# Two batches' output projection kept transposed, and five reorderings at the two ends of a transformer block

## The chip, the cores and the metric

The kernel runs on one core of one Trainium2 chip. Its time is the device time of one execution in microseconds (us), and a version's time is the median of its runs. The core has TensorE (matrix products, PE in the profile), VectorE (DVE), ScalarE (ACT), GpSimd (POOL) and SyncE (SP), each with an instruction queue of its own, processed in order; semaphores alone hold one engine to another.

## What is computed

One pre-norm transformer layer on x of 4 batches x 1024 tokens x 128 channels, 16 heads of 64 channels:

```python
x = x + attn(layernorm(x))          # attn adds its own input: h + z, h = layernorm(x)
#   q, k, v = h @ w_q, h @ w_k, h @ w_v            per head
#   z = softmax(q k^T / 8) v, heads side by side, @ w_o
x = x + moe(layernorm(x))
#   router: softmax(xf @ Wr), one expert of 8 for each token, at most 512 tokens an expert
#   y = p * relu(xe @ W1[e]) @ W2[e], put back at the token's row
```

## The kernel before

**Attention.** The heads are done two at a time: a pair `j` (0 to 31, `LAST` = 31, eight pairs `HP` a batch) is worked in four parts called `oct`, two for each half `h` of 512 queries. In an oct TensorE makes eight score tiles (keys standing, 512 queries moving; lines 1367 and 1368) that ScalarE exponentiates into `ring` (L831), multiplies them with the values (`values`, L1383, 16 instructions), and makes two visits of plain scores for the next pair (`max_scores`, L1315). VectorE takes the maxima of these visits (`reduce_max`, L1054). GpSimd adds the exponentiated tiles up for the softmax sums (`add_up`, L662, seven additions of 128x1024 a half); TensorE turns them into sums with a product with ones (`softmax_sums`). VectorE inverts the sums (`recip`, L1059), and `scale_z` (L1068) multiplies z by them. In the last half of the last pair TensorE itself sums the last `LAST_BY_PE` = 2 tiles (`sums_by_pe`, L1391), and GpSimd adds the others.

**Output projection.** `project_out(j, h, bank)` (L1410) runs two pairs later, in octs 1 and 3 (one in each oct of the last pair): four products with a 128x128 tile of z standing and the 128x128 weights `wo` moving, which give rows of tokens. `add_out` (L1070, its addition L1074) adds that bank to the residual rows `x2`. PE's next visit waits for it (`wo_added`), as the bank is one half of the visit's bank. In oct 3 of a pair and in oct 1, `turn_max` (L1348) transposes the maxima behind it.

**The start.** VectorE takes the moments and the inverse roots of the first batch (`inverse_root`: a first guess and three Newton steps of three instructions, L947 to L949, each awaited by the next), then normalises; TensorE transposes and projects, and makes the first visits of pair 0 (`first_visit`) one by one as VectorE frees the banks. `turn_max(0, 0, ps_z)` follows `first_visit(4, 0)`.

**The end.** In `pair` of VectorE, `scale_z(LAST - 2, 0)` stands in oct 3 of pair 30, and `scale_z(LAST - 2, 1)` and `scale_z(LAST - 1, 0)` in oct 0 of the last pair behind the second two maxima. ScalarE's copy of the sums of pair 30 (`copy_sums_out`, L822) waits for the latter, as both use `sums`, and TensorE's third score tile of oct 1 waits for that copy, as the bank is the same. After the last pair TensorE makes router logits of the last batch's first half (L1437), runs `sums_by_pe`, `count_ranks` (L1478 to L1484), `softmax_sums` (L1406), then `end_project` and `end_turn_sums`; VectorE's `end_half(1)`, `end_root(1)` and `choose(B, ...)` follow, and with the slots found GpSimd scatters the last tokens (L632). TensorE meanwhile centres W1 (L1666), spins on products nobody reads (L1265) and transposes the first expert's tokens (L1679).

**The experts.** ScalarE casts the transposed tokens to the high part (`xeT_split`), VectorE makes the remainder (`low_tokens`, `xeT_ready`). For each of four chunks TensorE adds three products: low weights x high tokens, high weights x low tokens, high x high (L1705 to L1707), all behind `xeT_ready`.

What sets the order around the change is written out by hand: `pair` of each engine says what stands where in each oct.

Of the kernel before, what the change touches and what calls it, by code (L numbers as in the profile page):

```python
# [25 lines left out]
def block_kernel(nc, x_in, w_q, w_k, w_v, w_o, w_r, w_1, w_2, out):  # L26
# [31 lines left out]
    with ExitStack() as ctx:  # L58
# [62 lines left out]
        sums = sb("sums", [P, HALF])  # L121
        mxw = [sb(f"mxw{i}", [P, 2 * HT]) for i in range(2)]
# [79 lines left out]
        wo_added = sem("wo_added")  # L202
        sums_turned = sem("sums_turned")
# [92 lines left out]
        LAST_BY_PE = 2  # L296
# [70 lines left out]
        assert all(ROUTE_FROM + 2 * b >= HP * (b + 1) + 1 for b in range(1, B - 1)) and ROUTE_FROM + 2 * B + 2 <= PAIRS  # L367

# [565 lines left out]
        def _(dve):  # L934
# [11 lines left out]
            def newton(v, y, t):  # L946
                then(dve.scalar_tensor_tensor(out=t, in0=y, scalar=-0.5, in1=y, op0=ALU.mult, op1=ALU.mult))  # L947
                then(dve.tensor_tensor(t, t, v, ALU.mult))
                return dve.scalar_tensor_tensor(out=y, in0=t, scalar=1.5, in1=y, op0=ALU.add, op1=ALU.mult)  # L949
# [15 lines left out]
            def inverse_root(n, c):  # L965
# [4 lines left out]
                for _ in range(3):  # L970
                    then(newton(v, y, t))
# [134 lines left out]
            def end_root(h):  # L1106
# [4 lines left out]
                then(newton(v, y, t))  # L1111
                then(newton(v, y, t))

            def end_root_done(h):
                n, c = 2 * B - 1, slice(h * HT, (h + 1) * HT)
                v, y, t = (roots[:, n, k, c] for k in range(3))
                newton(v, y, t).then_inc(root_ready, 1)
# [8 lines left out]
            def pair(j, par, b):  # L1126
                nxt = 1 - par
                first, last = known(j, 0), known(j, LAST)
                for oct in range(OCTS):
# [19 lines left out]
                    if oct >= 2 and not known(j, LAST - 1, LAST):  # L1149
                        low_qk(j + 2, oct - 2)  # L1150
                    if outputs(j, oct) is not None:
                        add_out(*outputs(j, oct), lent_out)
# [105 lines left out]
        def _(pe):  # L1258
# [229 lines left out]
            def pair(j, par, b):  # L1488
# [3 lines left out]
                for oct in range(OCTS):  # L1492
# [38 lines left out]
                    for made in tiles:  # L1531
                        if made[2] is not lent_max:
                            project_tile(*made)
                    if outputs(j, oct) is not None:
# [199 lines left out]
```

## Time and profile before

| | |
|---|---|
| median of 3 runs | 1509.79 us (1508.08 to 1510.36) |
| the profiled execution | 1508.29 us, its span 1506.2 us |
| busy share PE, POOL, DVE, ACT | 98%, 81%, 66%, 52% |
| chain that ended last | PE 87%, POOL 5%, DVE 3%, issue 2% |
| granted clock of TensorE, mean | 0.995 |

A row of the trace's timeline gives start and duration in us, engine, line, operation, tiles and the count of merged instructions; the brackets give idle time of that engine before it and who ended it. An f32 product is two instructions in these records (x8 for the four products of `project_out`), one with both operands f32r is one. Durations of neighbouring products overlap, so what a product costs is read from starts.

### The profile page before, as it was taken

The page shows a single profiled execution, that of the slowest core. Times are in us where ns is not written, and L with a number is a line of the kernel's source. Part 1 is how long each engine was busy: PE and PEld are TensorE (multiplying, and loading weights), DVE is VectorE, ACT ScalarE, POOL GpSimd, SP SyncE. Part 2 cuts the span into 40 slices and gives each one's busy share as a digit, 9 for nine tenths or more (in the row PEclk, how much of TensorE's full clock was granted, in tenths as well). Part 3 has the DMA queues.
Part 4 walks back from the last instruction along what each step waited for, and adds up shares of the span by engine and source line. Part 5 has one row for each costly group of instructions (what it writes and reads, how often), then busy time and mean ns, then how long its engine had stood idle before and what let it go on. Part 6 is the DMA issues. An engine that isn't in the chain of part 4 may idle for free.

```text
span 1506.2 us, 21680 instructions
## 1 busy us (share of the span) xinstructions
PE 1478.4 (98%) x7244; PEld 841.6 (56%) x7244; DVE 995.8 (66%) x1228; ACT 784.5 (52%) x1540; POOL 1216.1 (81%) x675
## 2 busy tenths in 40 slices
PE   8999999999999999999999999999999999998897
PEld 5555555555555555555555555555655556554586
DVE  6557666676777656766666657676677666677543
ACT  4565556565555554555455555555555455453331
POOL 5888778898798878888778878889789998899535
PEclk9999999999999999999999999999999999999999
DMA  6334444442343434332444433333444423440431
GB/s 149 90 81 93 94 113 108 107 104 60 82 104 88 114 83 108 87 83 65 95 98 100 114 83 90 86 76 89 98 96 96 107 72 79 103 107 12 133 84 34
DMA packets 125294, 137.88 MB, mean 92 GB/s; under 512 B 44107, under 2 KB 69198, under 8 KB 125185
## 3 DMA queue, kind: packets, MB, share of 16 engines
q1 hardware_dynamic: 118784, 130.26, 37.3%
q0 software_dynamic: 2048, 4.10, 0.9%
q10 hardware_dynamic: 4352, 2.13, 0.5%
q8 instruction: 59, 0.97, 0.3%
q14 instruction: 51, 0.41, 0.1%
HBM read 16.81 MB, written 8.45 MB: 17 GB/s over the span
## 4 chain that ended last, share of the span: by engine, by line
PE 87%; POOL 5%; DVE 3%; issue 2%; ACT 1%; SPq 1%; DMA 1%; POOLq 0%; ACTq 0%; DVEq 0%
PE ps_w L1383 27%; PE ps_w L1367 16%; PE ps_w L1368 14%; PE ps_m L1315 10%; POOL acc L662 4%; PE ps_m L1416 3%; PE ps_w L1401 2%; PE ps_m L1283 2%; PE ps_m L1284 2%; PE ps_m L1285 2%; DVE mxw L1054 1%; PE ps_w L1690 1%; DVE z L1068 1%; PE ps_m L1690 1%; PE ps_m L1300 1%
## 5 line engine op out<-in xcount | busy, mean ns | idle before, releaser
L662 POOL TENSOR_TENSOR acc<-acc,ring 128x1024 f32<-128x1024 f32 x382 | 918.9, 2406 | 50.9 <-ACT ring L831 3.3
L1054 DVE TENSOR_REDUCE mxw<-ps_m 128x1 f32<-128x1024 f32 x512 | 601.4, 1217 | 323.3 <-PE ps_m L1315 312.3
L831 ACT ACTIVATE ring<-ps_w 128x512 f32<-128x512 f32 x1024 | 544.8, 600 | 253.5 <-PE ps_w L1368 235.9
L1383 PE MATMUL ps_w<-ring,V 128*64 128x512 f32 x2048 | 467.7, 598 | 0.0
L1367 PE MATMUL ps_w<-queriesA,keysA 128*128 128x512 f32 x1024 | 431.9, 422 | 5.1 <-ACT sums L822 2.8
L1368 PE MATMUL ps_w<-queriesB,keysB 65*128 65x512 f32 x1024 | 406.9, 397 | 0.0
L1383 PEld LDWEIGHTS ps_w<-ring,V 128*64 128x64 f32 x2048 | 135.7, 136 | 265.5 <-issue 234.9
L662 POOL TENSOR_TENSOR acc<-ring 128x1024 f32<-128x1024 f32 x64 | 152.2, 2378 | 157.4 <-PE ps_w L1401 150.5
L1367 PEld LDWEIGHTS ps_w<-queriesA,keysA 128*128 128x128 f32 x1024 | 194.0, 189 | 106.1 <-issue 48.6
L1368 PEld LDWEIGHTS ps_w<-queriesB,keysB 65*128 65x128 f32 x1024 | 194.7, 190 | 33.6 <-issue 0.7
L1315 PE MATMUL ps_m<-keysA,queriesA 64*128 64x512 f32 x1000 | 183.0, 444 | 1.2 <-issue 0.5
L1315 PEld LDWEIGHTS ps_m<-keysA,queriesA 64*128 64x128 f32 x1000 | 74.5, 184 | 149.6 <-issue 138.2
L811 ACT ACTIVATE z<-ps_w 128x512 f32<-128x512 f32 x64 | 38.3, 598 | 217.6 <-PE ps_w L1383 217.6
L1045 DVE TENSOR_TENSOR qk_rest<-ps_m,qk_high 128x512 fp32r<-128x512 f32 x123 | 85.1, 692 | 93.1 <-ACT qk_high L769 81.3
L1059 DVE RECIPROCAL sums<-sums 128x128 f32<-128x128 f32 x128 | 119.7, 940 | 0.0
L822 ACT ACTIVATE sums<-ps_w 128x512 f32<-128x512 f32 x33 | 19.7, 598 | 126.4 <-PE ps_w L1401 112.1
L1068 DVE TENSOR_TENSOR z<-by_sums,z 128x512 f32<-128x512 f32 x60 | 79.2, 1325 | 0.0
L769 ACT ACTIVATE qk_high<-ps_m 128x512 fp32r<-128x512 f32 x123 | 73.6, 598 | 8.7 <-DMA keysB<-qk_high 1.5
L1416 PEld LDWEIGHTS ps_m<-wo,z 128*128 128x128 f32 x496 | 65.8, 193 | 7.2 <-DVE mxw L1054 1.9
L1416 PE MATMUL ps_m<-wo,z 128*128 128x128 f32 x496 | 66.4, 277 | 1.1 <-DVE mxw L1054 1.1
L695 POOL DMA_INDIRECT out<-ye,ring x32 | 31.1, 971 | 35.2 <-DVE ye L1230 28.2
L1074 DVE TENSOR_TENSOR x<-ps_m,x 128x512 f32<-128x512 f32 x62 | 42.7, 688 | 23.5 <-PE ps_m L1416 23.5
(181 smaller groups left out, 981.3 us busy)
## 6 DMA issues: line engine op xcount, KB each, us to landing
queriesA<-qk_high SPq DMA_DIRECT2D x248, 128.0 KB
keysB<-qk_high SPq DMA_DIRECT2D x124, 128.0 KB
keysA<-qk_rest SPq DMA_DIRECT2D x124, 128.0 KB
queriesB<-qk_rest SPq DMA_DIRECT2D x124, 128.0 KB
by_sums<-sums SPq DMA_DIRECT2D x240, 64.0 KB, 2.0
keysA<-qk_high SPq DMA_DIRECT2D x93, 128.0 KB
tokens_by_slot<-blank ACTq DMA_DIRECT2D x16, 130.0 KB, 3.1
ring<-tokens_by_slot SPq DMA_DIRECT2D x8, 260.0 KB, 5.3
```

The costliest lines, as they stand in the source:

```text
L662: pool.tensor_tensor(acc[h][:, :], before, P_both(kt), ALU.add).then_inc(summed, 1)
L769: act.activation(qk_high[s][:, :], bank, ACT.Copy).then_inc(qk_cast, 1)
L831: act.activation(P_tile(kt, p), ps_s[k % 3][:, :], ACT.Exp, scale=SCALE).then_inc(exp_done, 1)
L1045: dve.tensor_tensor(qk_rest[s][:, :], qk_bank(j, use), qk_high[s][:, :].bitcast(F32), ALU.subtract).then_inc(qk_low, 1)
L1054: dve.tensor_reduce(mxw[h][:, p * HT + qt:p * HT + qt + 1], ps_m[p][:, :], AX_X, ALU.max).then_inc(maxed, 1)
L1059: dve.reciprocal(sums[:, c], sums[:, c]).then_inc(recip_done, 1)
L1068: dve.tensor_tensor(z[j % 2][h][:, :], by[:, :], z[j % 2][h][:, :], ALU.mult).then_inc(z_ready, 1)
L1315: mm = pe.matmul(ps_m[p][:, kh * HALF:(kh + 1) * HALF], queriesA[par][p][r, at:at + P], keysA[par][p][r, kh * HALF:(kh + 1) * HALF], start ...
L1367: pe.matmul(ps_s[k % 3][:, :], keysA[par][p][:, t], queriesA[par][p][:, c], start=True, stop=False)
L1368: pe.matmul(ps_s[k % 3][:, :], keysB[par][p][:, t], queriesB[par][p][:, c], start=False, stop=True).then_inc(scores_ready, 1)
L1383: mm = pe.matmul(ps_z[p * DK:(p + 1) * DK, :], V_of(j, kt, p), P_tile(kt, p), start=(kt == 0), stop=(kt == KT - 1))
L1416: mm = pe.matmul(bank[:, i * P:(i + 1) * P], z[j % 2][h][:, i * P:(i + 1) * P], wo[j % 3][:, :], start=True, stop=True)
```

## The change

1. **Output projection.** For pairs whose batch is 1 or 2 and that aren't the last of their batch (14 pairs, 28 halves), `project_out` makes one product with `wo` standing and 512 columns of z moving. The result is out transposed; VectorE sums it in `outT`, a view of `h_rows`, the first by a copy. In pairs 17 and 25, octs 1 and 2, `turn_back` (four transposes, by TensorE) turns a half of the sum and `add_back` (VectorE) adds it to the residual rows. The batch's last pair is added directly, behind `add_back`.
2. **`LAST_BY_PE`** is 1; after the last pair `softmax_sums` stands ahead of `count_ranks`.
3. **Roots.** Three Newton steps become one step of third order (four instructions) and one of second order (three), at the start and in `end_root`.
4. **`scale_z`** moves: for (29, 0) from oct 3 to oct 2 of pair 30; (29, 1) and (30, 0) ahead of the second two maxima of the last pair's oct 0.
5. **First visits.** `turn_max(0, 0, ps_z)` stands ahead of `first_visit(4, 0)`.
6. **Experts.** The two products with high tokens stand ahead of the one with low tokens; for expert 0 those of three chunks run ahead of the wait for `xeT_ready`.

```diff
-        LAST_BY_PE = 2
+        LAST_BY_PE = 1
+        outT = h_rows[:, :, :].rearrange("p t d -> p (t d)")
+        def transposed(j):
+            return 0 < j // HP < B - 1 and j % HP < HP - 1
+        def back(j, oct):
+            b, pair = divmod(j - HP - 1, HP)
+            return (b, oct - 1) if pair == 0 and 0 < b < B - 1 and oct in (1, 2) else None
...
-            def newton(v, y, t):
+            def third_order(v, y, t):
+                then(dve.tensor_tensor(t, y, y, ALU.mult))
                 then(dve.tensor_tensor(t, t, v, ALU.mult))
+                then(dve.scalar_tensor_tensor(out=t, in0=t, scalar=-10.0 / 3.0, in1=t, op0=ALU.add, op1=ALU.mult))
+                then(dve.scalar_tensor_tensor(out=y, in0=t, scalar=5.0, in1=y, op0=ALU.add, op1=ALU.mult))
+            def second_order(v, y, t):
+                ...
+                # three instructions, as newton had
...
             def add_out(j, h, bank):
                 b = j // HP
                 dve.wait_ge(wo_done, out_no(j, h))
+                if transposed(j):
+                    at = outT[:, h * HALF:(h + 1) * HALF]
+                    if j % HP > 0:
+                        dve.wait_ge(wo_added, out_no(j, h) - 2)
+                        dve.tensor_tensor(at, bank, at, ALU.add).then_inc(wo_added, 1)
+                    else:
+                        if b == 1:
+                            dve.wait_ge(residual_ready, B)
+                            dve.wait_ge(h_turned, 2 * B)
+                        else:
+                            dve.wait_ge(back_turned, 2 * b - 2)
+                        dve.tensor_copy(at, bank).then_inc(wo_added, 1)
+                    return
+                if 0 < b < B - 1:
+                    dve.wait_ge(back_added, 2 * b + h - 1)
+            def add_back(b, g):
+                dve.wait_ge(back_turned, 2 * b + g - 1)
+                dve.wait_ge(residual_ready, b + 1)
+                at = x_tiles(b, g * HT, HT)
+                dve.tensor_tensor(at, lent_turn.rearrange("p (t d) -> p t d", d=D), at, ALU.add).then_inc(back_added, 1)
...
+                    if last and oct == 0:
+                        scale_z(j - 2, 1)
+                        scale_z(j - 1, 0)
                     if oct == 2 and not (first or last or both):
                         recip(j - 1, 1, 3)
                     if not (last and oct >= 1):
...
                         reduce_max(v, h, qt, 1)
                         reduce_max(v, h, qt, 0)
-                    if oct == 0 and last:
-                        scale_z(j - 2, 1)
-                        scale_z(j - 1, 0)
-                    if oct == 3 and known(j, LAST - 1):
+                    if oct == 2 and known(j, LAST - 1):
                         scale_z(j - 1, 0)
...
+                if transposed(j):
+                    pe.matmul(bank, wo[j % 3][:, :], z[j % 2][h][:, :], start=True, stop=True).then_inc(wo_done, 1)
+                    return
...
+            def turn_back(b, g):
+                pe.wait_ge(wo_added, 2 * HP * (b + 1) - 2)
+                for i in range(g * HT, (g + 1) * HT):
+                    mm = pe.transpose(lent_turn[:, (i - g * HT) * P:(i - g * HT + 1) * P],
+                                      outT[:, i * P:(i + 1) * P], ident[:, :])
+                mm.then_inc(back_turned, 1)
...
-            first_visit(4, 0)
             pe.wait_ge(first_copied, 4)
             turn_max(0, 0, ps_z)
+            first_visit(4, 0)
...
             sums_by_pe(LAST, 1, range(KT - LAST_BY_PE, KT))
+            softmax_sums(LAST, 1, LAST_BY_PE)
             count_ranks(B - 1, lent_out)
-            softmax_sums(LAST, 1, LAST_BY_PE)
...
             for e in range(E):
+                ahead = 3 if e == 0 else 0
+                pe.wait_ge(xeT_split, e + 1)
+                for c in range(ahead):
+                    up_by_high(e, c)
                 pe.wait_ge(xeT_ready, e + 1)
                 for c in range(FC):
+                    if c >= ahead:
+                        up_by_high(e, c)
+                    up_by_low(e, c)
```

## Rows read from the trace of the kernel before

**Rows 1.** The page: busy time, share and instructions of each engine.
```profile
PE 1478.4 (98%) x7244; PEld 841.6 (56%) x7244; DVE 995.8 (66%) x1228; ACT 784.5 (52%) x1540; POOL 1216.1 (81%) x675
```

**Rows 2.** Timeline of PE: start, duration, engine, line, operation, tiles, count.
```profile
42.34 1.02 PE L1279 MATMUL ps_m<-hT,wst 128*128 128x512 f32 x2
...
43.43 0.40 PE L1368 MATMUL ps_w<-queriesB,keysB 65*128 65x512 f32 x1
...
443.17 0.40 PE L1368 MATMUL ps_w<-queriesB,keysB 65*128 65x512 f32 x1
443.41 0.60 PE L1270 MATMUL ps_m<-ident,h_rows 128*128 128x128 f32 x4
...
444.08 0.39 PE L1368 MATMUL ps_w<-queriesB,keysB 65*128 65x512 f32 x1
...
1396.99 1.05 PE L1416 MATMUL ps_m<-wo,z 128*128 128x128 f32 x8
...
1398.12 0.40 PE L1368 MATMUL ps_w<-queriesB,keysB 65*128 65x512 f32 x1
```

**Rows 3.** Timeline of PE, the last pair's octs 0 and 1.
```profile
1372.97 1.16 PE L1416 MATMUL ps_m<-wo,z 128*128 128x128 f32 x8 [1.05 <-DVE mxw L1054]
...
1385.21 0.50 PE L1367 MATMUL ps_w<-queriesA,keysA 128*128 128x512 f32 x1 [2.76 <-ACT sums L822]
```

**Rows 4.** Timeline of ACT in the last pair.
```profile
1384.56 0.60 ACT L822 ACTIVATE sums<-ps_w 128x512 f32<-128x512 f32 x1 [8.31 <-DVE z L1068]
```

**Rows 5.** Timeline of DVE from pair 30 to the last pair's oct 1.
```profile
1367.39 1.65 DVE L1068 TENSOR_TENSOR z<-by_sums,z 128x512 f32<-128x512 f32 x1
...
1378.50 3.19 DVE L1068 TENSOR_TENSOR z<-by_sums,z 128x512 f32<-128x512 f32 x1
1381.62 2.84 DVE L1068 TENSOR_TENSOR z<-sums,z 128x512 f32<-128x512 f32 x1
```

**Rows 6.** The instructions of line 1068: count, ns min/median/max, first and last start.
```profile
L1068 DVE TENSOR_TENSOR z<-by_sums,z x60: 678/1273/3193, 118.9 to 1378.5; 128x512 f32<-128x512 f32 x60
```

**Rows 7.** Timeline of POOL in the last pair.
```profile
1373.93 0.99 POOL L632 DMA_INDIRECT tokens_by_slot<-x,scatter_at  x1 [0.16 <-issue]
...
1378.77 2.37 POOL L662 TENSOR_TENSOR acc<-ring 128x1024 f32<-128x1024 f32 x1
1381.28 15.75 POOL L662 TENSOR_TENSOR acc<-acc,ring 128x1024 f32<-128x1024 f32 x6
1397.42 2.38 POOL L662 TENSOR_TENSOR acc<-ring 128x1024 f32<-128x1024 f32 x1 [0.40 <-ACT ring L831]
```

**Rows 8.** Busy time by stretch, us of PE, PEld, DVE, ACT, POOL, then PEclk.
```profile
1385.00:1391.00 6.00, 5.79 (x23) 4.51 (x25) 4.52 (x6) 3.96 (x9) 5.71 (x3) 0.72 0.00 0
```

**Rows 9.** Timeline of PE behind the last pair and at the first expert.
```profile
1414.42 1.06 PE L1437 MATMUL ps_m<-wr_centred,hT 128*128 128x8 f32 x8
1415.41 1.94 PE L1391 MATMUL ps_w<-ring,ones 128*64 128x512 f32 x8
...
1417.55 1.08 PE L1406 MATMUL ps_w<-acc,ones 128*64 128x512 f32 x4
...
1441.89 0.47 PE L1705 MATMUL ps_w<-xeT_high,w_low 128*128 128x512 f32 x1 [1.50 <-DVE xeT_low L1236]
```

**Rows 10.** Timeline of DVE behind the last pair.
```profile
1420.02 0.21 DVE L1082 RECIPROCAL end_scale<-ps_w 128x8 f32<-128x8 f32 x1 [0.96 <-PE ps_w L1447]
...
1425.31 0.16 DVE L949 SCALAR_TENSOR_TENSOR roots<-roots 128x4 f32<-128x4 f32 x1
1425.51 0.19 DVE L1001 TENSOR_REDUCE routing_columns<-ps_m 128x4 f32<-128x32 f32 x1
```

**Rows 11.** Timeline of PE at the start.
```profile
9.86 0.66 PE L1270 MATMUL ps_w<-ident,h_rows 128*128 128x128 f32 x4 [1.47 <-DVE h_rows L975]
...
28.47 0.73 PE L1326 MATMUL ps_m<-keysA,queriesA 64*128 64x512 f32 x2
29.13 0.50 PE L1367 MATMUL ps_w<-queriesA,keysA 128*128 128x512 f32 x1
```

More of the change, by code:

```diff
@@ L202, in block_kernel @@
         wo_added = sem("wo_added")
+        back_turned = sem("back_turned")
+        back_added = sem("back_added")
         sums_turned = sem("sums_turned")
@@ L944, in then @@
                 dve.wait_ge(chain, steps[0])
-            def newton(v, y, t):
-                then(dve.scalar_tensor_tensor(out=t, in0=y, scalar=-0.5, in1=y, op0=ALU.mult, op1=ALU.mult))
+            def third_order(v, y, t):
+                then(dve.tensor_tensor(t, y, y, ALU.mult))
                 then(dve.tensor_tensor(t, t, v, ALU.mult))
-                return dve.scalar_tensor_tensor(out=y, in0=t, scalar=1.5, in1=y, op0=ALU.add, op1=ALU.mult)
+                then(dve.scalar_tensor_tensor(out=t, in0=t, scalar=-10.0 / 3.0, in1=t, op0=ALU.add, op1=ALU.mult))
+                then(dve.scalar_tensor_tensor(out=y, in0=t, scalar=5.0, in1=y, op0=ALU.add, op1=ALU.mult))
+            def second_order(v, y, t):
+                left = 3.0 / 8.0
+                then(dve.scalar_tensor_tensor(out=t, in0=y, scalar=-0.5 * left ** 3, in1=y, op0=ALU.mult, op1=ALU.mult))
+                then(dve.tensor_tensor(t, t, v, ALU.mult))
+                return dve.scalar_tensor_tensor(out=y, in0=t, scalar=1.5 * left, in1=y, op0=ALU.add, op1=ALU.mult)
             def find_moments(n, b, g):
@@ L969, in inverse_root @@
                 then(dve.tensor_scalar(y.bitcast(I32), v.bitcast(I32), -0.5, float(0x5F3759DF), ALU.mult, ALU.add))
-                for _ in range(3):
-                    then(newton(v, y, t))
+                third_order(v, y, t)
+                then(second_order(v, y, t))
             def first_norm(g):
@@ L1110, in end_root @@
                 then(dve.tensor_scalar(y.bitcast(I32), v.bitcast(I32), -0.5, float(0x5F3759DF), ALU.mult, ALU.add))
-                then(newton(v, y, t))
-                then(newton(v, y, t))
+                third_order(v, y, t)
             def end_root_done(h):
@@ L1150, in pair @@
                         low_qk(j + 2, oct - 2)
+                    if back(j, oct) is not None:
+                        add_back(*back(j, oct))
                     if outputs(j, oct) is not None:
@@ L1533, in pair @@
                             project_tile(*made)
+                    if back(j, oct) is not None:
+                        turn_back(*back(j, oct))
                     if outputs(j, oct) is not None:
@@ L1573, in pair @@
                             pe.wait_ge(hT_ready, 2 * turn[0] + turn[1] + 1)
+                        if back(j, oct) is not None:
+                            b, g = back(j, oct)
+                            pe.wait_ge(back_added, 2 * b + g - 1)
                         if c is not None and oct < 2:
@@ L1697, in _, with up_by_high, up_by_low @@
             pe.wait_ge(w2_loaded, 16 * FC)
+            def up_by_high(e, c):
+                n, w = e * FC + c, slice(e * F + c * P, e * F + (c + 1) * P)
+                if n >= 3:
+                    pe.wait_ge(relu_done[(n - 3) % 2], (n - 3) // 2 + 1)
+                pe.matmul(up_bank(n), w1_low[:, w], xeT_high[e % 2][:, :], start=True, stop=False)
+                pe.matmul(up_bank(n), w1_high[:, w], xeT_high[e % 2][:, :], start=False, stop=False)
+            def up_by_low(e, c):
+                n, w = e * FC + c, slice(e * F + c * P, e * F + (c + 1) * P)
+                pe.matmul(up_bank(n), w1_high[:, w], xeT_low[e % 2][:, :], start=False,
+                          stop=True).then_inc(up_done, 1)
             for e in range(E):
+                ahead = 3 if e == 0 else 0
+                pe.wait_ge(xeT_split, e + 1)
+                for c in range(ahead):
+                    up_by_high(e, c)
                 pe.wait_ge(xeT_ready, e + 1)
                 for c in range(FC):
[L1701 to L1708 removed]
+                    if c >= ahead:
+                        up_by_high(e, c)
+                    up_by_low(e, c)
                 if e + 1 < E:
```

10 lines of the change are left out of this document (1 added, 9 removed).

## The prediction

> **What bounds the kernel now.** I read the busy shares first: TensorE (PE) is busy for 1478.4 of 1506.2 us [rows 1], so through most of the kernel a change is worth what it takes from PE's own stream. POOL stands second at 81%, which matters where PE becomes faster. Then I looked at what PE's stream costs in the middle, by distances between starts [rows 2], and then for the places where PE waits. These lie at the two ends. In the last pair PE waits 1.05 us for VectorE's maxima and 2.76 us for a copy by ScalarE [rows 3]; that copy had itself waited 8.31 us for `scale_z` [rows 4]. Behind the wait the granted clock is 0.72 of full over 6 us [rows 8], so part of that stretch ran at 1.2 instead of 2.4 GHz.
>
> **The wide projection, 28 times.** Three places are measured in the same way, from the start of the special product to the start of the second score product (L1368) behind it. For the narrow form it is 1398.12 - 1396.99 = 1.13 us [rows 2]. The wide form isn't in this kernel as an output projection, but `project_qk` of pair 1 is the same shape, 128x128 f32 standing and 512 f32 columns moving: 43.43 - 42.34 = 1.09 us [rows 2]. One projection thus gains 0.04 us, 28 gain 1.1 us. The reason is that both forms stream 512 columns in two instructions' worth of passes, and four small products pay hardly anything for their weight loads. Bounds of the wide price: 0.41 us lower if it took only as long as two f32r products of 512 columns (443.41 - 443.17 = 0.24 each [rows 2], 0.48 against 0.89 for the narrow set, which is 1.13 less one such 0.24), and as high as two whole durations, bounded by the first product's 1.02 us in the row of L1279 against that 0.89, 0.13 higher. I take 1.09, the row of equal shape.
>
> The Trainium skill (TensorE: Matmul & The Clock Gate, section Back-to-back issue gap) has streams of a weight load and a product each at about 81 ns for 128 columns and 131 ns for 512, which would make wide products far cheaper by the column. By it, as an estimate, eight narrow instructions are 0.65 us, two wide ones 0.26, and 28 projections would give 10.8 us instead of 1.1. The trace doesn't agree: its eight narrow ones take 0.89 us and its two wide ones 0.85.
>
> **Turning back, 4 times.** Four transposes by identity, measured alike: 444.08 - 443.41 = 0.67 us, less the 0.24 of the score product that lies between: 0.43 us [rows 2]. Four of them cost PE 1.7 us. With each comes an `add_back` on DVE, an addition with one PSUM operand that I price as `add_out`'s, 0.7 us. In octs 1 and 2 of pairs 17 and 25 it is queued ahead of `add_out` or `scale_z`, a reciprocal and two maxima; PE's next visit waits for it. DVE is 66% busy [rows 1], and PE itself reaches the visit 0.43 us later, so I take no wait; if DVE's queue has no room there, it is up to 0.7 each, 2.8 in all. The waits that `add_out` gains are for adds two places back, and once, in pair 10, for POOL's residual of batch 3, which is queued ahead of that pair's first addition; I take nothing for them. The middle: -1.1 + 1.7 = +0.6 us, bounds -9.8 (cheap wide products) and +8.1 (0.13 x 28 + 1.7 + 2.8).
>
> **`scale_z` in pairs 30 and 31.** Its price depends on POOL. Over 60 instances the least is 0.68 us and the median 1.27 [rows 6]; the two in the last pair took 3.19 and 2.84 [rows 5], under POOL's additions, which run on from 1378.77 [rows 7]. (a) `scale_z(29, 0)` took 1.65 us [rows 5] ahead of two reciprocals and the maxima for which PE then waited 1.05 us [rows 3]. Moved one oct up it is off that path, and DVE waits for PE's visits there, so it is hidden: -1.05 us. (b) The other two now stand behind `add_out` at 1373.7 (my shifted time) and ahead of the maxima. In that time, 1373.93 to 1378.77, POOL issues four scatters and adds nothing [rows 7], so I take 0.7 to 1.3 us each. They end at about 1376, the maxima behind them at 1378.6, and PE asks for these after `values` and the sums, at 1379.4. If both took 3 us, PE would wait some 2.5 us there. (c) The copy of the sums then finds z scaled, and PE's wait of 2.76 us [rows 3] goes. What is late next is the product of the sums itself, which ends before oct 1. (d) With the gap gone I expect the low clock behind it to go too: 6 x (1 - 0.72) = 1.7 us [rows 8]. Sum of the last pair: 1.05 + 2.76 + 1.7 = 5.5 us, so that `values` of the last oct end at 1414.42 - 5.5 = 1408.9 [rows 9].
>
> **POOL, now next.** POOL doesn't move with this: its additions of the first half run without a gap to 1397.03, its second half began after 0.40 us of waiting [rows 7], which goes. With `LAST_BY_PE` = 1 it has six additions instead of five, at 2.5 (1381.28 - 1378.77) to 2.62 us (15.75/6) [rows 7]: from about 1397.0 to 1412.2. PE needs one tile of sums less (half of 1.94 us) and would be ready at 1408.9 + 1.0 + 1.0 = 1410.9. So `softmax_sums` starts when POOL is done, 1412.2 against 1417.55 [rows 9]: -5.3 us, of which the reorder with `count_ranks` and the smaller `sums_by_pe` can show no more, because POOL ends last. `count_ranks` (0.27 us, from 1417.28 in the trace to 1417.55) now lies between the sums and `end_turn_sums`, for which `end_half(1)` waited [rows 10]: +0.2.
>
> **Roots.** Two instructions fewer at 0.20 us of spacing [rows 10]. In `end_root(1)` the logits' `choose` follows them at once [rows 10]: -0.4. In `end_root(0)` DVE waits for the logits afterwards: 0. At the start PE waits 1.47 us for the normalised rows [rows 11]: -0.4.
>
> **First visits.** The scores of pair 0 start right behind the last visit (28.47, 29.13, no idle time [rows 11]), and the visits wait for VectorE, not for `turn_max`: 0. If the placed maxima ended as late as the visits, up to 0.6.
>
> **Experts.** PE waited 1.50 us for the low tokens [rows 9]; some 0.8 of it, VectorE's subtraction and its signal, is now covered by six products. But the first chunk is complete only after seven products instead of three, and the fourth chunk needs its bank back from the relu: 0.3 to 0.5 us of it return. -0.3, from 0 to -0.7. The later experts wait as before.
>
> **Sum.** +0.6 - 5.3 + 0.2 - 0.4 - 0.4 - 0.3 = -5.6 us. The profiled execution took 1508.3 us, which gives 1502.7; the median of the runs is 1.5 us above that execution. I put the forecast between the two bases, at 1503.3.
>
> **Rivals.** *The last pair pays half.* (b) goes wrong: scaling in front of the maxima still meets POOL, PE waits 2.5 us for the second visit, and that gap keeps part of the low clock. For it: 3.19 and 2.84 in the trace. Against it: the scatters lie just there. Gain 5.6 - 2.5 = 3.1 and less, 1506.0. *The wide product is dearer than equal shape says*, at its bound of 0.13 more than narrow, and `add_back` finds no room: the middle costs 8.1, 7.5 more than forecast: 1510.8. It changes the sign when a wide product costs 0.2 us more than I take (5.6/28). This is the slower case; for it speaks only that the row of L1279 is from the start, against it that PE streams columns everywhere at the same pace. With half of that price the result is near zero. *The wide product is cheap*, as two f32r products: 28 x 0.41 = 11.5 instead of 1.1, so 1492.9. For it no row; the rule of the skill quoted above points there. *The order doesn't do what it says*: VectorE's moved steps change nothing, because the last pair is tied to POOL's additions already. Against it, POOL's sums of the first half end at 1397.03, and PE would need them at 1397.3. If POOL were 1 to 2 us slower, PE would wait there, but then `softmax_sums` at the end is later by the same: 1505.
>
> **How the numbers follow.** Forecast 0.66; half pay or POOL slower 0.17 (1505 to 1506); middle dearer by half 0.07 (about 1508); dearer in full 0.05; cheap wide products 0.05. A measurement of this kernel can tell about 0.2%, 3.0 us, from no change. Faster by more than that: most of the forecast (0.64), half of the second case (0.08), the cheap case (0.05): 0.76 with rounding. Slower: 0.06. Within: 0.18. The range is 1499.5 to 1507.5: the terms at their good ends (first visits 0.6, experts 0.4, less low clock at W1, the profile's base) below, the half paying case and the higher base above; it leaves out the cheap case and the two dear ones.
>
> **What would show it.** In the profile after: L1416 with x2 at 128x512 taking the same distance to the second L1368 (1.09 us), not 0.7 or 1.3; four sets of transposes from `outT` at 0.43; no 2.76 us wait of L1367 for `sums`, and no low clock near 1386; L1068 at 0.7 to 1.3 in the last pair's oct 0; POOL's last addition ending right before L1406; PE's wait at the first expert near 0.7. I am wrong if the middle, from 300 to 1330 us, is shorter or longer by over 2 us, or if L1406 behind the last pair starts less than 4 us earlier.

## The result, and the profile after

The changed kernel takes 1506.29 us (median of 20 runs, 1502.63 to 1510.25). The kernel before, run beside it, takes 1508.51 us (20 runs, 1506.41 to 1514.71). The ratio is 0.9978, 95% interval 0.9971 to 0.9986: faster by 2.1 to 4.4 us. It lies near the ratio of the means (1505.94 and 1509.13 us); the medians are only 2.2 us apart. The profiled execution took 1507.38 us, with a span of 1505.5 us. The forecast was 1503.3 us, a gain of 5.6 against the base of the sum. The direction is right and the time lies inside the range, but more than two of the forecast microseconds are missing. The trace shows where each went.

Busy times, from the page of the kernel after (compare rows 1):

```profile
PE 1479.8 (98%) x7088; PEld 826.5 (55%) x7088; DVE 1002.3 (67%) x1226; ACT 784.5 (52%) x1540; POOL 1217.6 (81%) x676
```

PE has 156 instructions fewer and is as busy as before. The count alone doesn't give the time here.

**The last pair.** The timeline of PE after (start, duration, engine, line, operation, tiles, count, and in brackets the idle time before with what ended it):

```profile
1379.41 0.73 PE L1361 MATMUL ps_m<-keysA,queriesA 64*128 64x512 f32 x4
1380.07 3.65 PE L1429 MATMUL ps_w<-ring,V 128*64 128x512 f32 x16
1383.55 1.03 PE L1452 MATMUL ps_w<-acc,ones 128*64 128x512 f32 x4
1384.51 0.73 PE L1361 MATMUL ps_m<-keysA,queriesA 64*128 64x512 f32 x4
1385.17 0.50 PE L1413 MATMUL ps_w<-queriesA,keysA 128*128 128x512 f32 x1
```

No row of it has an idle time in brackets. Before, there was one of 1.05 and one of 2.76 us [rows 3]. VectorE over the same time, and ScalarE's copy of the sums:

```profile
1378.12 0.69 DVE L1113 TENSOR_TENSOR x<-ps_m,x 128x512 f32<-128x512 f32 x1 [1.25 <-PE ps_m L1465]
1378.72 0.82 DVE L1092 TENSOR_TENSOR z<-by_sums,z 128x512 f32<-128x512 f32 x1
1379.47 0.68 DVE L1092 TENSOR_TENSOR z<-sums,z 128x512 f32<-128x512 f32 x1
1380.17 2.36 DVE L1078 TENSOR_REDUCE mxw<-ps_m 128x1 f32<-128x1024 f32 x2
```
```profile
1384.63 0.60 ACT L837 ACTIVATE sums<-ps_w 128x512 f32<-128x512 f32 x1 [4.43 <-PE ps_w L1452]
```

The two scalings take 0.82 and 0.68 us instead of 3.19 and 2.84 [rows 5]. ScalarE now waits for PE's product, no longer for z [rows 4]. The low clock behind the gap is gone: busy times of PE, PEld, DVE, ACT and POOL with their counts, then PEclk, DMA share and GB/s, which answer to rows 8:

```profile
1384.00:1390.00 6.00, 6.00 (x33) 3.99 (x29) 4.33 (x5) 3.98 (x9) 5.70 (x4) 1.00 0.03 11
```

I compared the starts of `values` oct by oct in both traces. The shift between them falls by 1.27 us at the last pair's oct 0 and by 4.50 us at its oct 1: 5.77 us, where the forecast had 1.05 and 2.76 + 1.7 (5.5 in all).

**Behind the last pair.** PE after (compare rows 9):

```profile
1413.88 1.06 PE L1493 MATMUL ps_m<-wr_centred,hT 128*128 128x8 f32 x8
1414.87 1.08 PE L1437 MATMUL ps_w<-ring,ones 128*64 128x512 f32 x4
1416.94 1.08 PE L1452 MATMUL ps_w<-acc,ones 128*64 128x512 f32 x4 [1.00 <-POOL acc L677]
1418.88 0.19 PE L1534 MATMUL ps_m<-one_hot_b,upper 128*128 128x32 bf16 x1 [0.85 <-DVE one_hot_b L1031]
```

The wait of 1.00 us for POOL was forecast: POOL ends last. The wait of 0.85 us for the one-hots wasn't. VectorE shows where it comes from, in `end_root(0)`, and POOL what runs beside it:

```profile
1410.88 1.05 DVE L1154 TENSOR_SCALAR roots<-moments 128x4 f32<-128x4 f32 x1
1411.96 0.17 DVE L1155 TENSOR_SCALAR roots<-roots 128x4 int32<-128x4 int32 x1
1412.16 2.25 DVE L964 TENSOR_TENSOR roots<-roots 128x4 f32<-128x4 f32 x1
1414.45 0.16 DVE L965 TENSOR_TENSOR roots<-roots 128x4 f32<-128x4 f32 x1
1414.64 2.27 DVE L966 SCALAR_TENSOR_TENSOR roots<-roots 128x4 f32<-128x4 f32 x1
1416.94 0.16 DVE L967 SCALAR_TENSOR_TENSOR roots<-roots 128x4 f32<-128x4 f32 x1
...
1417.62 0.19 DVE L1025 TENSOR_REDUCE routing_columns<-ps_m 128x4 f32<-128x32 f32 x1
```
```profile
1404.49 12.40 POOL L677 TENSOR_TENSOR acc<-acc,ring 128x1024 f32<-128x1024 f32 x5
```

An instruction on 128x4 elements takes 0.16 us, except three: the first takes 1.05 us, and two later ones take 2.25 and 2.27 us. Before, these roots ran while POOL had already finished, and all of them took 0.16 or 0.17:

```profile
1413.72 0.16 DVE L949 SCALAR_TENSOR_TENSOR roots<-roots 128x4 f32<-128x4 f32 x1
1415.52 0.19 DVE L1001 TENSOR_REDUCE routing_columns<-ps_m 128x4 f32<-128x32 f32 x1 [1.64 <-PE ps_m L1437]
```

So the roots had 1.64 us of room before, and now they are late. The product of the ranks starts 5.00 us behind the start of the logits (2.86 before), and the first W1 product 13.50 us (12.59 before): 0.9 us lost.

**The middle.** A wide product next to a set of turning products, and then PE and DVE at the first turning back (pair 17, octs 2 and 3):

```profile
1079.98 1.02 PE L1462 MATMUL ps_m<-z,wo 128*128 128x512 f32 x2
1080.85 0.60 PE L1480 MATMUL ps_m<-ident,x 128*128 128x128 f32 x4
```
```profile
788.00 0.60 PE L1472 MATMUL ps_m<-ident,h_rows 128*128 128x128 f32 x4
788.36 0.48 PE L1413 MATMUL ps_w<-queriesA,keysA 128*128 128x512 f32 x1
...
795.16 0.73 PE L1361 MATMUL ps_m<-keysA,queriesA 64*128 64x512 f32 x4 [0.91 <-DVE mxw L1078]
```
```profile
788.66 0.68 DVE L1119 TENSOR_TENSOR x<-ps_m,x 128x512 f32<-128x512 f32 x1
789.26 2.78 DVE L1092 TENSOR_TENSOR z<-by_sums,z 128x512 f32<-128x512 f32 x1
791.96 0.94 DVE L1083 RECIPROCAL sums<-sums 128x128 f32<-128x128 f32 x1
792.83 2.28 DVE L1078 TENSOR_REDUCE mxw<-ps_m 128x1 f32<-128x1024 f32 x2
```

The two instructions of one wide product take 1080.85 - 1079.98 = 0.87 us. The octs with one are shorter than before, by up to 0.05 us each; over the 28 this is 0.9 us (0.45 in pairs 10 to 16 and 0.42 in pairs 18 to 24, read in proj_only, which has no other change), where 1.1 was forecast. The turning costs more than forecast: the shift between the traces grows by 0.44, 0.27 and 0.96 us over octs 1 to 3 of pair 17, and by the same amounts in pair 25, 3.3 us in all instead of 1.7. `add_back` itself takes 0.68 us, as forecast (0.7). But it pushes `scale_z` to where that takes 2.78 us, and PE waits 0.91 us for the maxima behind it. The addition of POOL that `scale_z` meets there begins 0.15 us ahead of it:

```profile
789.11 2.38 POOL L677 TENSOR_TENSOR acc<-acc,ring 128x1024 f32<-128x1024 f32 x1
```

**Phases of low clock.** The shift also jumps by 3.05 us in pair 24, and this is no wait:

```profile
1091.84 0.95 PE L1493 MATMUL ps_m<-wr_centred,hT 128*128 128x8 f32 x8
...
1093.44 0.60 PE L1414 MATMUL ps_w<-queriesB,keysB 65*128 65x512 f32 x1
...
1095.97 5.77 PE L1429 MATMUL ps_w<-ring,V 128*64 128x512 f32 x16
```
```profile
1093.70:1100.50 6.80, 6.80 (x19) 2.26 (x20) 4.44 (x15) 1.49 (x3) 6.51 (x4) 0.52 0.05 13
```

For 6.8 us PE is busy throughout, but at the lower of its two levels (1.2 GHz; the granted clock is 0.52 of full), and `values` takes 5.77 us instead of 3.65. A shorter phase at 18 us (3.4 us) takes back the 0.48 us that the roots gave at the start and 1.1 more. Whether such phases belong to the change was the first thing to settle.

**The experts.** PE waits 0.78 us instead of 1.50 [rows 9], and 0.32 us come back behind the ninth product, ahead of the fourth chunk:

```profile
1441.70 0.47 PE L1763 MATMUL ps_w<-xeT_high,w_low 128*128 128x512 f32 x1 [0.78 <-ACT xeT_high L934]
...
1444.35 0.50 PE L1763 MATMUL ps_w<-xeT_high,w_low 128*128 128x512 f32 x1 [0.32 <-DVE rT L1296]
```

### The profile page after: what moved, and what is told of

The parts are those of the page before. It is cut to its first block, busy times and chain, and to the rows that moved or that the text cites. A ratio compares the mean times of both kernels' runs of the same rounds, so it can differ in the third digit from the quotient of the medians.

```text
span 1505.5 us, 21408 instructions
## 1 busy us (share of the span) xinstructions
PE 1479.8 (98%) x7088; PEld 826.5 (55%) x7088; DVE 1002.3 (67%) x1226; ACT 784.5 (52%) x1540; POOL 1217.6 (81%) x676
## 4 chain that ended last, share of the span: by engine, by line
PE 90%; DVE 4%; POOL 2%; ACT 1%; issue 1%; DMA 0%; POOLq 0%; ACTq 0%; DVEq 0%
PE ps_w L1429 28%; PE ps_w L1413 17%; PE ps_w L1414 15%; PE ps_m L1361 10%; POOL acc L677 2%; PE ps_w L1447 2%; PE ps_m L1465 2%; PE ps_m L1329 2%; PE ps_m L1330 2%; PE ps_m L1331 2%; PE ps_m L1462 2%; DVE mxw L1078 1%; PE ps_w L1751 1%; PE ps_m L1751 1%; PE ps_m L1346 1%
## 5 line engine op out<-in xcount | busy, mean ns | idle before, releaser
L1329 PE MATMUL ps_m<-h_high,w_low 128*128 128x512 f32 x120 | 47.6, 397 | 0.0
L1330 PE MATMUL ps_m<-h_low,w_high 128*128 128x512 f32 x120 | 47.3, 394 | 0.0
L1331 PE MATMUL ps_m<-h_high,w_high 128*128 128x512 f32 x120 | 47.2, 394 | 0.0
```

What stands on the lines that cost most here:

```text
L1329: pe.matmul(bank, w_low[par][:, w], h_high[:, c], start=True, stop=False)
L1330: pe.matmul(bank, w_high[par][:, w], h_low[:, c], start=False, stop=False)
```

## The experiments

Ten kernels ran, in three groups, each with runs of the kernel before beside it: medians 1509.5, 1510.12 and 1508.59 us. The mean granted clock of one execution scatters between 0.988 and 0.996, and within a kernel the span follows it, by 1.06 us per 0.001 (a line with one slope through all executions but one; the one left out, of proj_only, had a clock of 0.944 and a span of 1528.3 us, and would not lie on it). So beside each ratio I give the span read from that line at a clock of 0.994, "at equal clock". The kernel before has 1505.9 +- 0.1 us there, the changed kernel 1503.3 +- 0.2.

Such a figure takes away chance, but also what a change does to the clock itself. The phase of low clock behind the old gap in the last pair is in all four traces that have the old order of the scalings (the kernel before, before_again, proj_only, experts_only; 3.4 us, in proj_only 6.8) and in none of the eight with the new order, where PEclk is 1.00 from 1378 to 1396 us. 3.4 us at half clock are 1.7 us, or 0.0011 of the mean clock; by the line that is 1.2 us. As an estimate, the kernels with the new order are thus some 1.2 us better against the kernel before than their figures at equal clock say.

**before_again** is the kernel before, unchanged.

> The kernel before, unchanged, for the granted clock of each of its executions. Theory A (phases of low clock fall on any version, by where TensorE's idle and thin stretches happen to lie): ratio 1.000, the mean granted clock scatters between 0.991 and 0.996 from execution to execution, and the span follows it, about 1.5 us for each 0.001. Theory B (the change brought the extra low phases of the after trace, at 18 us and at 1094 us): the clock here is 0.995 in all executions, with the scatter of the spans unrelated to it.

Measured: 1508.77 us, ratio 0.9998 [0.9988, 1.0009], 1505.9 at equal clock. Its clocks reach from 0.990 to 0.995, nearly as far as those of the changed kernel, with spans from 1504.7 to 1511.6 us: theory A in that. The span follows less steeply than expected, 1.06 us per 0.001 and not 1.5. The trace itself shows no phase in the middle; its one at 1386 us (PEclk 0.57 over 1386 to 1390) is that of the gap in the last pair.

**ends_only** has the changes of order, and the projection as before (the diff is against the changed kernel):

```
         def transposed(j):
-            return 0 < j // HP < B - 1 and j % HP < HP - 1
+            return False
...
         def back(j, oct):
...
-            return (b, oct - 1) if pair == 0 and 0 < b < B - 1 and oct in (1, 2) else None
+            return None
...
-                if 0 < b < B - 1:
-                    dve.wait_ge(back_added, 2 * b + h - 1)
```

> The changed kernel with the output projection as it was before (no transposed sums, no turning back); the five reorderings stay. Theory A: the projection costs TensorE's stream 28 x -0.04 + 2 x 1.67 = +2.2 us, so this one is 2 us faster than the changed kernel, about 0.9965 of before; from pair 10 to pair 26 the distance to before stays constant. Theory B (the wide product is what keeps the clock down): also free of low phases in the middle, 0.9945. Rival C (the projection pays after all, by something the steps don't show): slower than the changed kernel, 0.998 or more.

Measured: 1502.87 us, ratio 0.9952 [0.9939, 0.9966], 1501.9 +- 0.5 at equal clock. The order alone gives more than the whole change: the two intervals don't meet. The ratio can't decide between A (0.9965) and B (0.9945), as its interval holds both. The trace speaks against B: it, too, has a phase of low clock in the middle, at 1091.5 us (PEclk 0.50 over 1091.5 to 1098), almost where the changed kernel has one, and it has neither wide products nor turning.

**proj_only** has the projection, and the order of before (all five edits at the ends undone).

> The kernel before with only the output projection changed. Theory A: +2.2 us by the steps of the trace (-0.04 in each oct with a wide product, +1.67 in each of pairs 17 and 25), ratio 1.0015. Forecast of the prediction: +0.6 us. Rival C: faster than before by 1 us or more.

Measured: 1511.53 us, ratio 1.003 [1.0004, 1.0056], 1507.9 +- 0.2 at equal clock: 2.0 us slower than before. By the steps in the trace it should be 3.3 - 0.9 = 2.4, and between pair 10 and pair 26 the trace's shift grows by 2.1. So eight of its ten executions need no effect on the clock to explain them. The other two stand out: 1517.78 us at a clock of 0.988 and 1530.28 us at 0.944, lower than any other execution on record. Neither was profiled, the 20 executions of the changed kernel, which has the same projection, reach no lower than 0.989, and why these two were so low is open.

**turn_late** is the changed kernel with the second turning back one oct later:

```
-            return (b, oct - 1) if pair == 0 and 0 < b < B - 1 and oct in (1, 2) else None
+            return (b, oct // 2) if pair == 0 and 0 < b < B - 1 and oct in (1, 3) else None
```

> The changed kernel with the second half turned back in oct 3 instead of oct 2. Theory A1 (in oct 2 the added step of VectorE pushes scale_z into GpSimd's next addition, where it takes 2.8 instead of 1.3 us, and the maxima behind it hold up TensorE's second visit by 0.91 us): pairs 17 and 25 cost 0.9 us each instead of 1.67, the wait of 0.91 us for the maxima is gone, 1.5 us less in all. Rival A2 (the turn costs what it costs wherever it is put): 1.67 each again, with the wait in oct 3.

Measured: 1504.83 us, ratio 0.9968 [0.9957, 0.9979], 1502.6 +- 0.3 at equal clock. In pairs 17 and 25 the steps of octs 1 to 3 are 0.44, -0.03 and 0.45 us: 0.87 a pair, twice PE's own 0.43, instead of 1.67. By its ratio alone it can't be told from the changed kernel; the trace decides. Its VectorE in the place of the rows above:

```profile
789.30 0.85 DVE L1092 TENSOR_TENSOR z<-by_sums,z 128x512 f32<-128x512 f32 x1
790.08 0.94 DVE L1083 RECIPROCAL sums<-sums 128x128 f32<-128x128 f32 x1
791.05 2.36 DVE L1078 TENSOR_REDUCE mxw<-ps_m 128x1 f32<-128x1024 f32 x2
```

This execution runs 0.64 us later there, POOL's additions with it. So `scale_z`, without an addition in front of it, starts 0.31 us before a running addition of POOL ends (789.61), and takes 0.85 us; in the changed kernel it started 0.15 us after the next one began. The extra 0.8 us a pair is thus VectorE's queue in oct 2 (theory A1), and most of what the addition does there is to push the scaling into POOL's next addition.

**scale_only** is the kernel before with the three scalings moved and nothing else:

```
+                    if last and oct == 0:
+                        scale_z(j - 2, 1)
+                        scale_z(j - 1, 0)
                     ...
-                    if oct == 0 and last:
-                        scale_z(j - 2, 1)
-                        scale_z(j - 1, 0)
-                    if oct == 3 and known(j, LAST - 1):
+                    if oct == 2 and known(j, LAST - 1):
```

> The kernel before with only the three moved steps of scale_z. Theory D (these moves are nearly the whole gain, and nothing behind the last pair takes it back as long as TensorE sums two tiles): values of the last pair's octs 0 and 1 come 1.26 and 5.76 us earlier, L1406 still starts 3.1 us behind the logits, ratio about 0.996. Rival E (GpSimd's additions take the gain back whatever LAST_BY_PE is): the logits are 5.8 us earlier, but L1406 starts over 4 us behind them, ratio 0.998.

Measured: 1503.3 us, ratio 0.9958 [0.9942, 0.9973], 1502.3 +- 0.6 at equal clock. The steps are -1.27 and -4.50 us, those of the changed kernel to the hundredth. The three moved lines give as much as all the changes of order in ends_only (0.9952) can be shown to give, and more than the whole change (theory D). One part of D was missed: L1406 starts 3.55 us behind the logits, between the 3.1 of D and the 4 of E. The roots of `end_root(0)` already meet POOL here, since everything of PE is earlier and POOL isn't: the ranks start 3.28 us behind the logits, and W1 13.00.

**pe2** is the changed kernel with `LAST_BY_PE` = 2.

> The changed kernel with LAST_BY_PE = 2 as before. Theory F (GpSimd's sixth addition keeps VectorE's instructions of end_root(0) waiting, 2.25 and 2.27 us for two of 0.16, so that the one-hots, the ranks and end_half(1) are late): GpSimd ends 2.5 us earlier, 0.5 us behind the start of the logits instead of 3.0; end_half(1) starts 5.7 to 5.9 us behind them instead of 6.7; 0.8 us faster than the changed kernel. Rival G (the order of softmax_sums and count_ranks is what costs): end_half(1) stays at 6.7, no gain, as TensorE has 0.9 us more to sum.

Measured: 1505.2 us, ratio 0.9969 [0.9956, 0.9982]. Its PE behind the last pair:

```profile
1412.39 1.06 PE L1493 MATMUL ps_m<-wr_centred,hT 128*128 128x8 f32 x8
1413.38 1.94 PE L1437 MATMUL ps_w<-ring,ones 128*64 128x512 f32 x8
1415.14 1.03 PE L1452 MATMUL ps_w<-acc,ones 128*64 128x512 f32 x4
1416.10 0.19 PE L1534 MATMUL ps_m<-one_hot_b,upper 128*128 128x32 bf16 x1
```

Both waits are gone, and POOL ends 0.52 us behind the start of the logits, as expected. From the logits to W1 it is 12.44 us instead of 13.50, so in the trace the sixth addition costs 1.1 us (theory F). The line at equal clock gives 1504.4 +- 0.7 and can't show so little.

**ends_pe2** is ends_only with `LAST_BY_PE` = 2.

> All that the steps of the traces say pays: the five reorderings with LAST_BY_PE = 2, and the output projection as it was. By theory A and F together: 2.1 us (projection) and 0.8 us (GpSimd) faster than the changed kernel, ratio to before 0.9948. If the parts don't add up (rival): 0.997, as the changed kernel.

Measured: 1503.88 us, ratio 0.9959 [0.9945, 0.9973], 1501.1 +- 0.5 at equal clock. In the trace W1 starts 12.23 us behind the logits, 1.3 earlier than in ends_only (13.52). By the ratios the two can't be told apart, and the interval holds both the expected 0.9948 and the rival's 0.997.

**experts_only** is the kernel before with the new order of the first expert's products.

> The kernel before with only the experts' order changed. Prediction: from the first transposes of tokens to the last product 0.3 us less than the 55.8 to 56.4 us of the kernel before; the wait for the first expert 0.8 instead of 1.5 us, a new one of 0.3 us in front of the fourth chunk. Rival: it is worth more, 0.7 us and over, because the later experts gain too.

One execution, 1509.15 us. PE waits 0.78 and 0.32 us there as in the changed kernel, and from the turning of the tokens to the last product it is 55.67 us. The other kernels with the old order have 56.44 (before), 55.75, 55.77 and 55.88, those with the new order 55.14 to 55.76. The gain of the wait, 1.50 - 0.78 - 0.32 = 0.4 us, is there; over the whole stretch it is no more than this scatter.

**split_add** and **ends_split** test what holds the tiny instructions up. POOL's additions of the last half are issued as two of half the width, in the changed kernel and in ends_pe2:

```
+                if known(j, LAST) and h == 1:
+                    half = slice(0, HALF)
+                    pool.tensor_tensor(acc[h][:, half], before[:, half], P_both(kt)[:, half], ALU.add)
+                    half = slice(HALF, 2 * HALF)
+                    pool.tensor_tensor(acc[h][:, half], before[:, half], P_both(kt)[:, half],
+                                       ALU.add).then_inc(summed, 1)
+                    return
```

> The changed kernel with POOL's additions of the last pair's second half (L677, 128x1024, 2.48 us each) issued as two of 128x512. Theory H: a VectorE instruction that reads two operands from SBUF waits for the end of POOL's running addition and is not slowed otherwise. Then no instruction of the first end root takes 2.25 us any more, but at most 1.3 (half an addition plus its own 0.16); there are more such waits, about one for each two root instructions; the roots are done about 6.0 us behind the start of the last logits instead of 6.8 less the logits, and the product of count_ranks starts at 4.0 to 4.6 us behind the logits instead of 5.00. POOL ends 0 to 0.5 us later (3.0 to 3.5 behind the logits). Rival R: two engines share the bandwidth, so a VectorE instruction beside an addition is slowed by a factor whatever the addition's length: then instructions of 2.2 us remain and count_ranks stays at 5.0. Median ratio to before 0.997 to 0.9985 in either case: this run is for the trace.

> The changes of order without the wide projection, two tiles of sums left to TensorE, and POOL's additions of the last pair's second half halved as in the other run. POOL ends at 0.6 to 1.0 us behind the start of the last logits (0.64 with whole additions). Theory H: the one wait of 2.25 us in the first end root becomes one or two of at most 1.3, count_ranks starts at 3.2 to 3.7 (3.72 before it), and the run gains 0 to 0.5 us on that of whole additions (ratio 0.9959): 0.9950 to 0.9960. Rival R: nothing moves.

Measured for split_add: 1505.27 us, ratio 0.9976 [0.9964, 0.9989]. VectorE and POOL:

```profile
1408.38 1.19 DVE L1162 TENSOR_SCALAR roots<-roots 128x4 int32<-128x4 int32 x1
1409.61 0.16 DVE L971 TENSOR_TENSOR roots<-roots 128x4 f32<-128x4 f32 x1
1409.81 1.17 DVE L972 TENSOR_TENSOR roots<-roots 128x4 f32<-128x4 f32 x1
1411.01 1.19 DVE L973 SCALAR_TENSOR_TENSOR roots<-roots 128x4 f32<-128x4 f32 x1
1412.24 0.16 DVE L974 SCALAR_TENSOR_TENSOR roots<-roots 128x4 f32<-128x4 f32 x1
```
```profile
1408.28 1.27 POOL L681 TENSOR_TENSOR acc<-acc,ring 128x512 f32<-128x512 f32 x1
1409.69 1.27 POOL L679 TENSOR_TENSOR acc<-acc,ring 128x512 f32<-128x512 f32 x1
1410.92 1.26 POOL L681 TENSOR_TENSOR acc<-acc,ring 128x512 f32<-128x512 f32 x1
1412.33 1.27 POOL L679 TENSOR_TENSOR acc<-acc,ring 128x512 f32<-128x512 f32 x1
```

The held instructions end at 1409.57, 1410.98 and 1412.20 us; POOL's additions end at 1409.55, 1410.96 and 1412.18. None takes over 1.19 us. A slowdown by a shared rate would have left some at 2.2. So theory H holds in this: such an instruction is held to the end of the addition that runs. The expected gain did not come. The rows show why: between the two halves of one tile POOL leaves no gap (1410.96 to 1410.92), and only behind the second one of 0.14 us (1409.55 to 1409.69, 1412.18 to 1412.33). The free instructions, L971 and L974, are the ones that start in such a gap. So there are five waits after the first instruction instead of two, the roots are no earlier, and the ranks start 5.22 us behind the logits (expected 4.0 to 4.6). POOL ends 0.8 us later for its twelve instructions. ends_split: 1504.59 us, ratio 0.9968 [0.9955, 0.9981], 1501.1 +- 0.1 at equal clock, the ranks at 3.72 as with whole additions. Its expectation of 0.9950 to 0.9960 was missed by the ratio. At equal clock it is level with ends_pe2: nothing gained, nothing lost, which is what rival R had said, though not for R's reason.

The three best ratios are those of ends_only, scale_only and ends_pe2: 0.9952, 0.9958 and 0.9959 against 0.9978 for the changed kernel. All three beat the kernel before; that they beat the changed kernel is clear of noise for ends_only only, as the other two intervals just reach its own.

## Why the prediction was nearly right, step by step

**The last pair was right, by its mechanism and by its size.** -5.5 forecast, -5.77 measured, and scale_only shows that the three moved lines do it alone. The two scalings met the last 0.27 us of an addition of POOL and its scatters (0.82 and 0.68 us; 0.7 to 1.3 forecast), and the low clock behind the gap went with the gap, in all eight traces without it.

**The wide product was right to the hundredth.** 0.04 us each was taken from the row of equal shape [rows 2], and 0.03 was measured, 0.9 us for the 28. The section Back-to-back issue gap of the Trainium skill (TensorE: Matmul & The Clock Gate) would have had, as an estimate from its figures, 10.8 us for the 28. The trace of the kernel after disagrees with it as that of before did: two instructions of 512 f32 columns take 0.87 us, four of 128 take 0.43.

**Turning back was mis-sized: 1.7 us forecast, 3.3 measured.** PE's part was right (0.43 a set, as turn_late's steps show). The term that failed is "PE itself reaches the visit 0.43 us later, so I take no wait". It used VectorE's mean busy share (66%) for one place. At that place the addition pushed `scale_z` from where it took 1.30 us to where it took 2.78, and with it the maxima. The 0.7 us for each turning, given there as a bound, is what oct 2 cost: 0.8 in each of the two pairs, 1.6 us in all.

**POOL as the next bound was right, and the roots behind it were overlooked.** That PE would wait for POOL at the sums is in the trace with 1.00 us. "In `end_root(0)` DVE waits for the logits afterwards: 0" is the step that failed. That room (1.64 us) existed because POOL had finished 3.64 us before the logits. With PE 5.8 us earlier in the last pair, and POOL with one addition more, POOL adds until 3.01 us behind their start, and the roots are held for 1.05 - 0.16 + 2.25 - 0.16 + 2.27 - 0.16 = 5.1 us. I had named that price in the same text for `scale_z` and didn't ask which other VectorE instructions would now run beside POOL. Cost: the forecast has W1 as far behind the logits as before (-5.5 at the logits, and -5.3 + 0.2 - 0.4 = -5.5 at W1), and the trace has it 0.9 us farther.

**The start was right in the wait (-0.48 us; -0.4 forecast), the experts in theirs (-0.4; -0.3).**

**The sum.** The forecast -5.6, with 1.6 more for the turning, 0.9 more at W1 and 0.2 more for the wide products, and with 0.3 less in the last pair and 0.1 less each at the start and the experts, is -3.4 us. The ratio says -3.3 (0.0022 x 1508.5), the line at equal clock -2.6 +- 0.3, or -3.8 with the 1.2 of the gap's own phase. The forecast time is off by 3.0 us: 2.3 by the gain, and 1.1 because the medians lie only 2.2 us apart and not 3.3, less 0.4 because the base was put at 1508.9 and came out at 1508.51.

**What was luck.** The time lies inside the range, but not by what the range allowed for. Its upper part, to 1507.5, stood for the last pair paying half and for the higher base; the last pair paid in full, and the two terms that came out dearer, the turning and the roots, were not in it. By the time alone, 1506.29, the rival at 1505 to 1506 would look right, and none of its mechanisms happened. Two of the signs of being wrong also show in the profiled execution as they are written: the middle is 4.2 us longer, and the product of the sums starts only 0.6 us earlier. 3.05 us of both are the low clock of pair 24, and the second also has the phase at 18 us in it. Without it the middle is 1.2 us longer, which would pass, and counted from the last pair on the product of the sums is 5.8 us earlier.

**What the clock did.** A comparison of the two profiled executions alone would have misled: they had clocks of 0.995 and 0.992, and at 1.06 us per 0.001 this is 3.2 us. The largest part of it in the two traces are the 3.05 us of pair 24. A phase in the middle is in three of the twelve traces: the changed kernel, turn_late (from 1180 us on) and ends_only (1091.5 us), so it needs no wide product. No kept trace with the old order has one there; that it falls on the kernel before too is inferred from the scatter of its clocks (0.990 to 0.995) and not shown. The phase near 18 us is shown on both: it is in eight of the twelve traces, and three of them (proj_only, scale_only, experts_only; PEclk 0.50 or 0.51 over 3.4 us) have the start of the kernel before. What sets such a phase off is open. In the three traces with one in the middle, logit products of 8 columns (L1493, or its like) lie within 2 us before it. These products are in every version and most of the time nothing follows, so this is a neighbourhood and not a cause. It wasn't tried.

## What to carry to other kernels

When a change makes one engine earlier against another, list every instruction that will now run beside the other's work, not only those that were moved: a piece that had 1.6 us of room can lose it to an engine that it never waits for by name. Price such an instruction by the rest of what is running there, up to one whole instruction of the neighbour. Shorter instructions of the neighbour only help if gaps stand between them. And judge the room in an engine's queue at the place where the new work is put, from the row that ends last there, never from a busy share of the whole.

## What the runs showed of the hardware

**A VectorE instruction beside a GpSimd addition can be held to the addition's end.** The roots wait for no semaphore of POOL there, so what the opening said, that semaphores alone hold one engine to another, is not so here. On 128x4 elements: 0.16 us alone, up to 2.27 beside additions of 2.4 us, at most 1.19 beside those of half the width (1.27 us), each time ending 0.01 to 0.02 us behind the addition (L1161 of split_add, 0.38 us, 0.03). `scale_z` obeys it too: in the row of 2.78 us it started at 789.26, and POOL's addition ended at 781.54 + 9.95 = 791.49, 2.23 us later; the remaining 0.55 is its own work. In the trace of the changed kernel 49 of the 62 scalings start while an instruction of POOL on two tensors runs, and each of them ends 0.55 to 0.63 us behind it; the other 13 start beside none, and take 0.68 or 0.69. So a scaling costs 0.55 us plus the rest of what POOL is at, and at least 0.68. The 60 of them with `by_sums` take 0.68 to 2.78 us (count, then min/median/max in ns), while `add_out`, of the same size but with one operand in PSUM, stays within 13 ns:

```profile
L1092 DVE TENSOR_TENSOR z<-by_sums,z x60: 678/1294/2779, 120.1 to 1378.7; 128x512 f32<-128x512 f32 x60
...
L1113 DVE TENSOR_TENSOR x<-ps_m,x x34: 681/692/694, 132.1 to 1410.3; 128x512 f32<-128x512 f32 x34
```

The Trainium skill (GPSIMD Engine Reference, Specifications) says that GpSimd shares its SBUF interfaces with VectorE and that contention is with VectorE instructions that read two inputs from SBUF or run in a two-port mode. The trace agrees where it can be seen: the additions with an operand in PSUM are never held (the row of L1113), and `scale_z`, with both operands in SBUF, is. The held L1154 and L1162 read one tensor, which fits only if they run in the second kind; no run here shows the mode. That the wait lasts to the end of the other's instruction is read here from the rows.

**What starts in a gap between two additions goes free.** POOL's additions in the changed kernel end at 1411.90 and 1414.39 us, and the next ones start at 1412.04 and 1414.54. L1155 (1411.96) and L965 (1414.45) start in these gaps and take 0.17 and 0.16 us; L964 and L966 start 0.1 us after an addition began and are held for the whole of it. In split_add it is the same: L971 and L974 start in gaps, and L973 after the begin of the second half, which follows the first without a gap. One case doesn't fit: the 3.19 us of [rows 5] started 0.26 us ahead of an addition [rows 7], behind a scatter, and was held to its end all the same. Four more traces have one such scaling each, 0.24 to 0.28 us ahead of an addition, and none of them tells why. With additions half as long there were more holds, and their sum stayed: the roots took 1414.95 - 1407.97 = 7.0 us in split_add and 1417.62 - 1410.88 = 6.7 in the changed kernel.

**The granted clock drops for some microseconds with PE busy throughout**: for 6.8 us in the row shown, and for 3.4 us near 18 us in kernels with the old start and the new. The span of an execution goes with its mean clock (1500.7 us at 0.996 to 1508.3 us at 0.989 for the changed kernel); that such phases make most of the scatter is likely, and not shown, as one execution of each kernel was profiled.
